# Reciprocal norms and a variance addition moved from VectorE to GpSimdE in a fused two-attention, two-feed-forward block

## The reference, cut to what matters

```
x = x + attn_a(layernorm(x))        # latent attention, 16 heads, causal softmax
x = x + ffn(layernorm(x))           # token-shift mix, sigmoid gate, squared relu
x = x + attn_b(layernorm(x))        # attention with l2-normalised q and k, 16 heads of 8
x = x + ffn(layernorm(x))

def layernorm(x): return (x - mean) / sqrt(var + 1e-5)

def attn_b(x):
    q, k, v = x @ Wq, x @ Wk, x @ Wv                 # heads of d = 8
    q = q / max(sqrt(sum(q * q)), 1e-12)             # the same for k
    return (softmax(causal(8 * q @ k.T)) @ v) @ Wo
```

## Time and profile before

| | |
|---|---|
| median of 3 runs | 1093.65 us (1092.25 to 1094.22) |
| span of the profiled execution | 1091.2 us |
| PE busy | 943.4 us, 86% |
| DVE busy | 877.4 us, 80% |
| ACT busy | 768.8 us, 70% |
| POOL busy | 282.1 us, 26% |
| chain that ended last | PE 44%, DVE 31%, ACT 16%, issue 6%, POOL 1% |

### The profile page before, as it was taken

How to read it: one execution, slowest core, us unless ns; L and a number is a source line. 1 busy time by engine, 2 the same in 40 slices (tenths; PEclk the granted TensorE clock), 3 DMA queues, 4 the chain that set the end, 5 groups by cost and what they waited for, 6 DMA issues and landing times.

```text
span 1091.2 us, 37281 instructions
## 1 busy us (share of the span) xinstructions
PE 943.4 (86%) x15889; PEld 514.4 (47%) x15889; DVE 877.4 (80%) x2112; ACT 768.8 (70%) x1042; POOL 282.1 (26%) x264
## 2 busy tenths in 40 slices
PE   3687979788989899999999999998989999899694
PEld 1333444444544445454554545454545555455352
DVE  3977777879789898989899898989898888864633
ACT  2165567667767778787777778787777778788681
POOL 6101123223223131312323132222223222222212
PEclk9988889999999999999999999999999999999897
DMA  5244414444517163452617162543618171405230
GB/s 145 70 104 100 118 36 94 118 126 112 146 44 196 28 167 80 131 126 82 174 45 195 38 181 56 151 105 99 158 61 196 36 181 41 111 11 127 67 62 20
DMA packets 94342, 112.95 MB, mean 104 GB/s; under 512 B 15200, under 2 KB 81888, under 8 KB 94176
## 3 DMA queue, kind: packets, MB, share of 16 engines
q1 hardware_dynamic: 94176, 110.56, 39.8%
HBM read 55.22 MB, written 54.53 MB: 101 GB/s over the span
## 4 chain that ended last, share of the span: by engine, by line
PE 44%; DVE 31%; ACT 16%; issue 6%; POOL 1%; DMA 1%; SPq 0%; POOLq 0%; DVEq 0%; ACTq 0%
PE acc L729 14%; DVE rowmax L1081 12%; ACT prob L930 10%; PE pool L712 6%; PE pool L595 4%; PE pool L643 4%; PE pool L762 3%; DVE xn L1039 3%; PE pool L609 2%; PE pool L784 2%; DVE stats L1027 2%; PE pool L770 2%; PE pool L659 2%; PE pool L681 2%; DVE rest_k L1052 2%
## 5 line engine op out<-in xcount | busy, mean ns | idle before, releaser
L930 ACT ACTIVATE prob<-pool 128x1024 f32<-128x1024 f32 x576 | 565.3, 1029 | 135.6 <-PE pool L659 132.1
L1081 DVE TENSOR_REDUCE rowmax<-pool 128x2 f32<-128x1024 f32 (+7 forms) x480 | 357.5, 792 | 66.7 <-PE pool L659 63.9
L729 PE MATMUL acc<-prob,vals_a 128*32 128x512 f32 (+7 forms) x2048 | 168.2, 424 | 0.2 <-ACT prob L930 0.2
L729 PE MATMUL acc<-prob,vals_b 128*32 128x512 f32 (+7 forms) x2048 | 162.9, 419 | 1.5 <-DVE turned_b L1116 1.1
L643 PE MATMUL pool<-stack_ka,stack_qa 48*64 48x512 bf16 (+7 forms) x2048 | 116.6, 300 | 40.9 <-ACT prob L930 12.7
L712 PE MATMUL pool<-stack_qa,stack_ka 51*64 51x512 bf16 (+7 forms) x2048 | 113.4, 301 | 32.7 <-DVE rowmax L1081 18.7
L659 PE MATMUL pool<-mask_t,ident_b 64*64 64x128 bf16 (+1 forms) x2304 | 129.7, 215 | 0.0
L712 PE MATMUL pool<-stack_qb,stack_kb 48*64 48x512 bf16 (+7 forms) x2048 | 112.2, 295 | 17.3 <-ACT prob L930 8.3
L643 PEld LDWEIGHTS pool<-stack_ka,stack_qa 48*64 48x64 bf16 x2048 | 42.7, 107 | 132.1 <-issue 45.9
L1291 POOL TENSOR_TENSOR rstd<-mv,minus_half 128x4 f32<-128x4 f32 x64 | 65.4, 1022 | 146.0 <-DVE mv L1034 146.0
L712 PEld LDWEIGHTS pool<-stack_qa,stack_ka 51*64 51x64 bf16 x2048 | 42.9, 108 | 88.5 <-issue 27.7
(11 more groups left out here) (129 smaller groups left out, 1374.4 us busy)
## 6 DMA issues: line engine op xcount, KB each, us to landing
stack_qa<-scratch_qa SPq DMA_DIRECT2D x64, 192.0 KB, 5.1
stack_ka<-scratch_ka SPq DMA_DIRECT2D x64, 192.0 KB, 5.7
stack_kb<-scratch_kb SPq DMA_DIRECT2D x64, 192.0 KB, 3.9
stack_qb<-scratch_qb SPq DMA_DIRECT2D x64, 192.0 KB, 4.8
scratch_qa<-parts_q SPq DMA_DIRECT2D x16, 384.0 KB, 2.9
scratch_ka<-parts_k SPq DMA_DIRECT2D x16, 384.0 KB, 4.3
scratch_qb<-parts_q SPq DMA_DIRECT2D x16, 384.0 KB, 2.6
scratch_kb<-parts_k SPq DMA_DIRECT2D x16, 384.0 KB, 2.7
```

Source lines behind the costliest of these rows:

```text
L729: last = eng.matmul(acc[32 * j:32 * j + 32, BLK * blk:T], vals[a][:, blk, GROUP * g + j, :], prob[n % NPROB][:, k, at:at + T - BLK * blk], ...
L930: eng.activation(prob[n % NPROB][:, :, :], place["unit", n][0][:, :, :], ACT.Exp, scale=scale).then_inc(S["exped"], 1)
L1081: last = eng.tensor_reduce(to, of, axis=AX.X, op=ALU.max)
```

## The change

Four edits:

1. Sums of squares: DVE's two reductions go; POOL adds halves in place in `qk` (512, 256, then 128 elements of output per partition, the last into `ssum`) and clamps `ssum`. The semaphore `norms2` now counts four instructions per batch.
2. The guess stays on DVE, waits for POOL's four instructions, and counts on a new semaphore `guess`. The Newton steps go to POOL: a third-order step (six instructions) and a second-order one (four), all 128 x 128, seven of them with two tensors and three with one. `turn_qk` on DVE waits for the tenth.
3. `var + 1e-5` goes from DVE to POOL, directly ahead of the power.
4. Part 1 of the maxima is made from the maxima and part 0 by an operation of two tensors, as `mrest` is, no longer by a copy of `mrest`, and doesn't wait for `mrest`.

The slots aren't changed.

```diff
 # class Vector
             def layernorm(self, b, n, src, ready, by):
...
-                q.wait_ge(S["mv" + n], b + 1)
-                eng.tensor_scalar(m[:, :, 1], m[:, :, 1], EPS, None, ALU.add).then_inc(S["var" + n], 1)
                 yield
...
                 eng.scalar_tensor_tensor(mr, mx, -1.0, mp[0], ALU.mult,
                                          ALU.subtract).then_inc(S["mrest"], 1)
+                eng.scalar_tensor_tensor(mp[1], mx, -1.0, mp[0], ALU.mult,
+                                         ALU.subtract).then_inc(S["mpart1"], 1)
                 q.wait_ge(S["mrest"], n)
-                eng.tensor_copy(mp[1], mr).then_inc(S["mpart1"], 1)
                 q.wait_ge(S["mpart1"], n)
...
             def project_qk(self, b):
+                yield
+                yield
-                    last = eng.tensor_reduce(
...
+            def rsqrt(self, b):
+                eng, q = self.eng, self.q
+                q.wait_ge(S["norms2"], 4 * (b + 1))
+                eng.tensor_scalar(rnorm[:, :].bitcast(mybir.dt.int32), ssum[:, :].bitcast(mybir.dt.int32),
+                                  -0.5, float(0x5f3759df), ALU.mult, ALU.add).then_inc(S["guess"], 1)
+                yield
+                yield
+                yield
...
 # class Pool
             def layernorm(self, b, n, src, ready, by):
...
+                var = mv[n][:, :, 1]
                 q.wait_ge(S["xn" + n], b)
+                q.wait_ge(S["mv" + n], b + 1)
+                eng.tensor_scalar(var, var, 1.0, EPS, ALU.mult, ALU.add).then_inc(S["var" + n], 1)
                 q.wait_ge(S["var" + n], b + 1)
...
             def rsqrt(self, b):
+                eng, q = self.eng, self.q
+                wide = qk[:, :, :, :].rearrange("p k a c -> p (k a) c")
+                n, w = 4 * b, C // 2
+                q.wait_ge(S["raw_qk"], 2 * (b + 1))
+                for level in range(2):
+                    q.wait_ge(S["norms2"], n + level)
+                    eng.tensor_tensor(wide[:, :, 0:w], wide[:, :, 0:w], wide[:, :, w:2 * w],
+                                      ALU.add).then_inc(S["norms2"], 1)
+                    w //= 2
...
+                eng.tensor_tensor(total, wide[:, :, 0:w], wide[:, :, w:2 * w], ALU.add).then_inc(S["norms2"], 1)
+                q.wait_ge(S["norms2"], n + 3)
+                eng.tensor_scalar(ssum[:, :], ssum[:, :], 1e-24, None, ALU.max).then_inc(S["norms2"], 1)
+                yield
+                r, t, u = rnorm[:, :], step_r[:, :], poly[:, :]
...
+                q.wait_ge(S["guess"], b + 1)
+                eng.tensor_tensor(t, r, r, ALU.mult).then_inc(S["newton"], 1)
...
+                yield
...
+                eng.tensor_tensor(r, r, u, ALU.mult).then_inc(S["newton"], 1)
                 yield
```

More of the change, by code:

```diff
@@ L277, in build @@
         step_r = sb("step_r", [P, NT * 2 * HEADS])
+        poly = sb("poly", [P, NT * 2 * HEADS])
         acc = pb("acc", [P, BANK])
@@ L305, in build @@
                      "mpart0", "mrest", "mpart1", "mpart2", "max_turned_ps", "max_turned", "max_rows0", "max_rows1",
-                     "scored", "exped", "weighed", "x_a", "qk_made", "raw_qk", "norms2", "newton", "qk",
+                     "scored", "exped", "weighed", "x_a", "qk_made", "raw_qk", "norms2", "guess", "newton", "qk",
                      "yT", "wo_made", "x_b"):
@@ L1066, in row_maxima @@
                 eng, q = self.eng, self.q
-                q.wait_ge(S["mrest"], 2 * (b - 1) + g + 1)
+                q.wait_ge(S["mpart1"], 2 * (b - 1) + g + 1)
                 for i, (step, u) in enumerate(units):
@@ new lines, in rsqrt @@
+                q.wait_ge(S["newton"], 10 * b)
+                q.wait_ge(S["norms2"], n + 2)
+                total = ssum[:, :].rearrange("p (k h) -> p k h", h=HEADS)
+                eng.tensor_tensor(total, wide[:, :, 0:w], wide[:, :, w:2 * w], ALU.add).then_inc(S["norms2"], 1)
+                q.wait_ge(S["norms2"], n + 3)
+                eng.tensor_scalar(ssum[:, :], ssum[:, :], 1e-24, None, ALU.max).then_inc(S["norms2"], 1)
+                yield
+                r, t, u = rnorm[:, :], step_r[:, :], poly[:, :]
@@ new lines, in rsqrt @@
+                n = 10 * b
+                q.wait_ge(S["guess"], b + 1)
+                eng.tensor_tensor(t, r, r, ALU.mult).then_inc(S["newton"], 1)
+                q.wait_ge(S["newton"], n + 1)
+                eng.tensor_tensor(t, t, ssum[:, :], ALU.mult).then_inc(S["newton"], 1)
+                q.wait_ge(S["newton"], n + 2)
+                eng.tensor_scalar(u, t, 0.375, -1.25, ALU.mult, ALU.add).then_inc(S["newton"], 1)
+                q.wait_ge(S["newton"], n + 3)
+                eng.tensor_tensor(u, u, t, ALU.mult).then_inc(S["newton"], 1)
@@ new lines, in rsqrt @@
+                q.wait_ge(S["newton"], n + 4)
+                eng.tensor_scalar(u, u, 1.0, 1.875, ALU.mult, ALU.add).then_inc(S["newton"], 1)
+                q.wait_ge(S["newton"], n + 5)
+                eng.tensor_tensor(r, r, u, ALU.mult).then_inc(S["newton"], 1)
+                yield
+                q.wait_ge(S["newton"], n + 6)
+                eng.tensor_tensor(t, r, r, ALU.mult).then_inc(S["newton"], 1)
+                q.wait_ge(S["newton"], n + 7)
+                eng.tensor_tensor(t, t, ssum[:, :], ALU.mult).then_inc(S["newton"], 1)
@@ L1375, in rsqrt @@
+                q.wait_ge(S["newton"], n + 8)
+                eng.tensor_scalar(u, t, -0.5, 1.5, ALU.mult, ALU.add).then_inc(S["newton"], 1)
+                q.wait_ge(S["newton"], n + 9)
+                eng.tensor_tensor(r, r, u, ALU.mult).then_inc(S["newton"], 1)
                 yield
```

26 lines of the change are left out of this document (1 added, 25 removed).

## The result

| | before | after |
|---|---|---|
| median of 4 runs | 1093.47 us | 1161.79 us (1161.13 to 1163.51) |
| span of the profiled execution | 1091.2 us | 1159.3 us |
| ratio of times | 1 | 1.0632, 95% interval 1.0619 to 1.0645 |

The change makes the kernel 6.3% slower. The prediction was 1118.6 us, with a range of 1101 to 1131. Its direction was right; its size was too small by 43 us. The difference of the spans, 68.1 us, is what the rest of this document accounts for.

A forecast was written before the change was run, and what follows sets the result against it. DVE and PE, both near full and handing work to each other, bound the kernel. Nine regular batches at +2.5 (+22.5) and the others (+2.5) made 1091.2 + 25 = 1116.2 profiled, 1118.6 us as median; range 1101 to 1131.

The forecast's parts named there:

- the sign named: Regular batches: the repeat of 60.6 us would become about 63 from guess to guess if the forecast was right.
- Parts 3 and 4: Variance addition on POOL: 0.2 us won per batch; part 1 of the maxima: 0.1 per batch, 1.6 us in all.
- Rival (a): Guess reaches DVE early enough, so relief of DVE wins: 1073 us; chance 0.09.
- (b): Hold at the guess mostly absorbed in PE's idle time, about 1 us per batch stays: 1104 us; chance 0.13.
- (d): Gains and hold cancel, within 0.2% of the time before: 1093.65 us; chance 0.04.
- rival (c): POOL's small operations cost as much as the power, lengthening sums and turn_qk's wait: 1176 us; chance 0.06.
- sums and clamp at 2.6 us: POOL's four instructions behind ffn_act take 2.6 us, so the row maximum after the guess is 3.45 us late.
- the delay has gone from 3.45 to 2.9: From first to later row maximum, removed Newton steps give back 0.55 us; with other gains, 2.5 us per regular batch.
- The row maximum at 683.9: Row maximum behind ffn_prod and the statistics, forecast to start at 683.9 instead of 681.00.
- the 0.2 of part 3: Gain of 0.2 us per batch from moving the variance addition, at the layer norm between ffn_prod and the row maximum.
- together +2.5: Batches outside 4 to 12: 0 to 2 win 3 us, the others lose a little; +2.5 us in all.
- 1.9 us of lateness: Hold of the row maximum after the guess below which the change would be faster than the kernel before.

The follow-up runs named there:

- e1: The changed kernel with POOL's sums and clamp moved ahead of ffn_act: 1119.74 us, ratio 1.0254 to the kernel before.
- e12: The kernel before, with POOL filling an unused tile behind ffn_act in batches 4 to 13 and DVE's clamp waiting for it: 1147.67 us, ratio 1.0531.
- e2_sums_only: The kernel before with only the sums and clamp moved to POOL, Newton steps still on DVE: 1176.40 us, ratio 1.0768.
- e3_newton_only: The kernel before with only the Newton steps moved to POOL, sums, clamp and guess still on DVE: 1089.73 us, ratio 0.9976.
- e10b: e1 with one wait added, so POOL starts ffn_act only after DVE's guess: 1105.83 us, ratio 1.0128 to the kernel before.
- e9: e1 with DVE's guess one slot later, behind a row maximum, at the second step of rsqrt: 1100.01 us, ratio 1.0083 to the kernel before.
- e11: The kernel before with the Newton steps and the variance addition on POOL, sums and maxima as before: 1083.48 us, ratio 0.9946.
- e7: The changed kernel with DVE's guess moved from the first to the third step of rsqrt: 1117.11 us, ratio 1.0226 to the kernel before.

## Why the prediction was right in sign and wrong in size

**What held.** The reading of the earlier trace rows carried: POOL's sums start at 640.38, directly behind ffn_act; the forecast had 674.4, less the offset 640.5. DVE sits idle 7.85 us before the guess (some 7 were forecast). The Newton steps run from 644.01 to 648.73, 4.7 us against 4.1, and end before the qk product. The regular batch went from about 61 us to 65.8, where about 63 was the sign named. POOL's busy time is 407.7 us against 390. Part 1 of the maxima is still near 0.9 us. Parts 3 and 4 came out as small as costed (2.4 us won, and nothing measurable instead of 1.6). Rival (a) is refuted, and so are (b), by which most of the hold would be absorbed, and (d), by which gains and hold would cancel. The measured time lies nearer to rival (c), 1176 us, than to the forecast, but not by its mechanism: POOL's small operations take 0.30 to 0.53 us and not the 1.02 of the power, and in the regular batches the qk product doesn't wait for them.

**The first term of the sum, sums and clamp at 2.6 us.** They take 643.70 - 640.38 = 3.32 us. Groups on POOL of the kernel after (count, busy us, mean ns, idle before):

```profile
L1363 POOL TENSOR_TENSOR qk<-qk 128x512 f32<-128x512 f32 x16 | 20.3, 1272 | 11.7 <-ACT raw L975 11.7
...
L1363 POOL TENSOR_TENSOR qk<-qk 128x256 f32<-128x256 f32 x16 | 11.6, 725 | 1.3
L1371 POOL TENSOR_SCALAR ssum<-ssum 128x128 f32<-128x128 f32 x16 | 8.5, 531 | 1.4
...
L1369 POOL TENSOR_TENSOR ssum<-qk 128x128 f32<-128x128 f32 x16 | 7.3, 455 | 2.5 <-POOL qk L1363 0.4
...
L1380 POOL TENSOR_SCALAR poly<-step_r 128x128 f32<-128x128 f32 x16 | 4.9, 306 | 1.4
```

128 elements of two tensors take 0.455 us (I took 0.33), 256 take 0.725 (0.55), the clamp 0.531 (0.25), and the first level, 512 elements, 1.272 (1.05). The rule "time goes with elements" from the earlier trace rows has too little fixed cost in it, and `affine_select` was a poor neighbour for an operation of two tensors. For the 512 elements a nearer row was at hand: x_ffn of the earlier trace rows takes 1.30 us, while the 1.05 are of ffn_act, which multiplies a tile by itself. That makes the row maximum 4.1 us late instead of 3.45: 0.6 us, or about 6 us of the 68.

**The step "the delay has gone from 3.45 to 2.9", and then to 2.5.** This is the first step that failed. The forecast let TensorE come out of its wait as it had gone in. The part of it about DVE came true: without Newton steps between them the row maxima give back 0.6 us (4.1 late at the first, 3.5 at the third). But TensorE had stood idle for 4.03 us, and what it did behind that ran at the lower clock: scores of 0.64 us where 0.41 was counted on, T_v's products of 1.63 instead of 1.16. So ffn_prod is 4.5 us late again, and from guess to guess it is 4.9. In all PE is busy 23.5 us longer. The Trainium skill (TensorE: Matmul & The Clock Gate, section "HAM oscillation — how this bites in real kernels") describes a kernel in which a wait in every repeat of a loop makes every repeat begin at the lower clock. This trace agrees, with VectorE in the place of a DMA: 0.72 to 0.86 in the 12 us behind the guess, in each regular batch.

The price of the clock can be read where the hold is equal. DVE waits 7.84 to 7.86 us before each of these guesses. Behind those of batches 7, 8 and 11 the granted clock is 0.86, and the way to the next guess is 4.5 to 4.6 us longer than before; behind those of batches 5, 6, 9, 10 and 12 it is 0.72 to 0.74, and the way is 5.1 to 6.0 us longer. (Batch 4 has 0.86 and only 3.1 us more, but its way was 62.2 us before, not 60.6.) In e1 the fall from 1.00 to 0.86 costs 1.6 us. As an estimate from these numbers, 1.6 to 2.7 of the 4.9 us are the clock's, and the rest is about the 2.5 forecast and the 0.6 of the longer sums. The regular batches took 44.4 us more where 22.5 were forecast. In e12 (no relief) 4.2 us late cost 66.47 - 60.93 = 5.5 us a batch, 1.3 us for each.

The sum has two slips of its own, both small. The row maximum at 683.9 already leaves out DVE's addition, so the 0.2 of part 3 is taken off twice (1.8 us over nine batches). And 1118.6 less 5 and 4 is 1109.6, not 1107.

**The batches outside, "together +2.5".** This is the second step that failed, and it is as large as the first: 21 us. From guess to guess the two traces give: to batch 1 -2.5; to batch 2 +5.3; to 3 +4.4; to 4 +6.3; from 13 to 14 +4.5; to 15 +2.4; to the end +3.3. Together +23.7. The runs with single parts say whose they are:

| us against before | to batch 1 | batch 1 to 4 | batch 13 to the end |
|---|---|---|---|
| after | -2.5 | +16.0 | +10.2 |
| `e2_sums_only` | 0.0 | +17.6 | +10.9 |
| `e3_newton_only` | +0.1 | +0.8 | +1.4 |

So it is mostly the sums on POOL. The forecast had let batches 0 to 2 win a microsecond each, since ffn_act isn't between there. But the four instructions take 3.3 us wherever they stand: DVE waits 6.60 us for them at the guess of batch 2, and 8.92 at that of batch 3, where ffn_diff is ahead of them. Moving them ahead of ffn_act and guarding the guess (e10b) leaves 10.3 of the 23.7 us.

Timeline of the kernel after in batch 1, of the kernel before at the same place, and of the last batch after:

```profile
213.45 1.26 POOL L1348 TENSOR_TENSOR x_ffn<-x_a,ffn_prod 128x512 f32<-128x512 f32 x1
...
214.75 0.87 DVE L1028 BATCH_NORM_STATS2 stats<-x_ffn 128x6 f32<-128x128 f32 x4 [4.08 <-POOL x_ffn L1348]
```

```profile
216.87 0.87 DVE L1027 BATCH_NORM_STATS2 stats<-x_ffn 128x6 f32<-128x128 f32 x4
```

```profile
1082.24 0.62 ACT L975 ACTIVATE raw<-pool 128x512 f32<-128x512 f32 x1
...
1086.27 0.23 DVE L1175 TENSOR_SCALAR rnorm<-ssum 128x128 int32<-128x128 int32 x1 [4.55 <-POOL ssum L1371]
...
1091.33 1.29 DVE L1187 TENSOR_TENSOR qk<-raw,rnorm 128x512 f32<-128x512 f32 x2 [4.83 <-POOL rnorm L1395]
```

In batch 1 x_ffn stands on POOL behind the ten Newton instructions, and DVE's statistics wait 4.08 us for it. It looks like the loss and isn't: the statistics start 6.35 us behind the guess (208.40), and 5.99 before (guess at 210.88), when DVE made its Newton steps in that time. In the last batch the way from the second copy (1082.86) to qk (1091.33) is 8.47 us, against 5.44 before and 7.2 forecast, by the same small operations.

**The value of the relief.** The forecast set the point from which rival (a) decides at 1.9 us of lateness. It lies far lower: e10b, with all the relief and 0.8 us late, is at 61.00, even with before. With no hold the relief is worth 0.4 to 0.7 us a batch (e9, e3, e11). Two Newton steps on DVE's chain in the earlier trace rows looked like 1.7 us; taken out, TensorE is waited for in their place, at 92% busy in e11's window.

**Open.** e9 and e10b are in the regular batches as quick as before or quicker, yet 0.8 and 1.3% slower in all. Their guess of batch 4 comes 3.4 and 3.9 us later than before, and from the guess of batch 12 to the end they need 7.5 and 6.6 us more. No experiment was made on those stretches alone, so what the sums delay there, and how much of it is the clock, stays open.

## What to carry to other kernels

Before work is moved to an engine with much idle time, read what stands ahead of the new place in that engine's queue and what that instruction waits for; then read what is queued behind the wait on the engine that was relieved. Price the hold by what stands idle behind it: where TensorE loses its clock over the wait in every repeat, a microsecond of hold costs more than a microsecond (5.5 us for 4.2 in e12). And price the first and the last repeats by themselves: here they made a third of the loss. Move only the parts whose results have slack: here the Newton steps and the addition, 0.5% faster, while the sums between a late input and an early user cost 7.7%.

## What the runs showed of the hardware that was not expected

An operation on DVE that starts just behind a POOL operation can stand still until that one ends. In the kernel before, the cast of part 1 showed this. The runs add two: the guess, 128 x 128 with a single tensor as input, takes 1.05 us instead of 0.23 (e1; 0.49 in e9, where it starts later beside ffn_act), and the pair of qk products 2.35 instead of 1.28 (e7). In e10b one added wait keeps POOL's start behind the guess and wins 14 us. The Trainium skill (GPSIMD Engine Reference, section 8, Key points) names contention with instructions in a 2-port mode or with two SBUF inputs. Of the qk product, which has two, the trace agrees. The guess has one input; it would have to be in a 2-port mode, which no row here shows.

POOL's clamp, a maximum with one constant, takes 0.531 us, while the multiply-and-add of the same shape takes 0.306 (L1380).
